# A token recurrence in 64 pairs instead of 56, with its planes stored pair by pair and the order of four engines rewritten around it

## The chip, the cores and the metric

One NeuronCore of a Trainium2 chip runs the whole program in one launch. The metric is device microseconds of one execution. Before the change three runs gave 447.07, 447.06 and 449.86 us, median 447.07 us. The engines are named as in the profile: PE (TensorE, with PEld for its weight loads), DVE (VectorE), ACT (ScalarE), POOL (GpSimd) and SP (SyncE, which only issues DMAs here).

## The reference, cut to what matters

1,536 tokens (8 images of 64 patches and 128 text tokens) are embedded, and then pass a recurrent layer, an expert layer with routing, a linear attention and a second expert layer. The change touches the recurrent layer alone:

```
def step(h, xs):
    b_t, d_t, u_t = xs                      # bivector, decay, injection of token t
    h_new = d_t * rodrigues(b_t, h) + u_t   # rotate the 64 3-vectors of a sequence, scale, add
    return h_new, h_new
_, states = scan(step, 0, tokens 0..191)    # 8 sequences of 192 tokens
```

`b_t`, `d_t` and `u_t` are projections of the layer-normed token. One step is an affine map of a 3-vector, so it can be written as a 3x4 matrix: nine entries from the rotation (through a quaternion) times the decay, and the injection as the fourth column. The map of two neighbouring tokens together is again one 3x4 matrix.

## The kernel before, in words

The 512 chains (8 sequences x 64 vectors) lie as 128 partitions x 4 (`NCH`). Time is cut into three chunks of 64 tokens (`TCH`): chunk 0 holds the patches, chunks 1 and 2 the text. For each chunk the planes bivector, angle, sine, cosine, quaternion and at last the entries of the matrices are computed with 256 elements a partition for a plane. `Mt` holds the matrices, `entries(c, sl)` is the view through which planes are written into it.

The work is spread over engines by a hand-written order; semaphores tie it together.

- **Chunk 0** is DVE's (L1303 to L1331): angles, reciprocal (`recip_of`, L536), products of two planes at a time, and at the end seven instructions that write the nine rotation entries (L1326, L1329, L1330). The last raises `m_ready` to 1.
- **Chunks 1 and 2** start with the projections on PE (`project`, L2110), copies of the bivector on ACT (L916), the squares (`squares_of`, L493, ACT), two additions on POOL (`theta2`, L486), the sigmoid's end on POOL (L685, for both chunks at once), square roots, sine and cosine on ACT, the quaternion on POOL (`quaternion`, L663). PE then adds up the entries in PSUM (`assemble`, L2192: the diagonal group first, then three off-diagonal groups in banks 5, 6 and 4), and ACT copies them into `Mt` (`keep_diagonal`, `keep_off`), which raises `m_ready`.
- **The recurrence** is DVE's, and serial. One step (`product` and `total`, L1342 to L1356) is four small instructions, two for each half of the chains: multiply the matrix entries by the state, and reduce. The states stand in a ring of two PSUM banks, and ACT copies every 32 of them to `hist` (`keep_states`). `steps` does one token each. `pair_steps` does two tokens each, with composed matrices: 0 to 79 were single steps and the other 112 tokens were 56 pairs in seven blocks of eight (`PBLK`), 136 steps in all.
- **The composed matrices** of a block come from POOL, which multiplies the terms (L715, nine instructions a block), PE, which sums them in PSUM (`pair_sums`, L2175), and ACT, which copies them (`keep_pairs`, L956, raises `pair_ready`). DVE waits for `pair_ready` at the head of each block.
- **The odd tokens** that a pair skips are filled in afterwards: the first 41 by POOL in three groups (L722 to L729), the last 15 by DVE (L1413, L1417).
- **What follows** needs all states: PE transposes them back into rows (L2270) once `odd_ready` (POOL and DVE) and `hist_copied` are complete; then come the layer norm, the routing and the experts.

`keep_busy` (L1870) issues matmuls whose result nobody reads. One count of them stands in front of `assemble`: 24 at L2172. The layer norm of the last four text tiles is four ACT instructions (`ln_norm(1, 2, h)`, L904); the text projections need them.

Of the kernel before, what the change touches and what calls it, by code (L numbers as in the profile page):

```python
# [29 lines left out]
ALU = mybir.AluOpType  # L30
# [3 lines left out]
P = 128  # L34
# [3 lines left out]
NJ = NTOK // P  # L38
# [26 lines left out]
PBLK = (8,) * 7  # L65
# [36 lines left out]
def build(nc, x, out):  # L102
    ctx = ExitStack()
    with ctx:
# [112 lines left out]
        Mt = mraw.rearrange("p (t a r c) -> p t a r c", a=NCH, r=3, c=4)  # L217

        Mf = mraw.rearrange("p (t a e) -> p e a t", a=NCH, e=12)
        hist = carve(reg1, (T + 1) * NCH * 4).rearrange("p (a c t) -> p t a c", a=NCH, c=4)  # L220
        biv = carve(reg1, 3 * NCH * T).rearrange("p (c a t) -> p c a t", c=3, a=NCH)
        dec = carve(reg1, NCH * T).rearrange("p (a t) -> p a t", a=NCH)
        U = NCH * TCH

        def unit(v, n):
            return v.rearrange("p (c a t) -> p c a t", c=n, a=NCH)
# [29 lines left out]
        ODD = (0, 8, 24, 41)  # L256
# [18 lines left out]
        comp += [of_pairs(setA.v.rearrange("p c a t -> p (c a t)"), 0, PBLK[6])]  # L275
        PAIR_BANK = (0, 6, 7, 4, 5, 6, 7)
        dodd = of_pairs(setA.trig.rearrange("p c a t -> p (c a t)"), 0, PAIRS - NODD)
# [93 lines left out]
        xn_ready = sem("xn_ready"); xn5_ready = sem("xn5_ready")  # L371
# [61 lines left out]
        biv0 = psum[:, 2 * 512:2 * 512 + 3 * U].rearrange("p (c a t) -> p c a t", c=3, a=NCH)  # L433
        dec0 = psum[:, 4 * 512 + 3 * U:6 * 512].rearrange("p (a t) -> p a t", a=NCH)
        inj0 = psum[:, 4 * 512:4 * 512 + 3 * U].rearrange("p (c a t) -> p c a t", c=3, a=NCH)
# [3 lines left out]
        RECIP_AT = 18  # L439
# [34 lines left out]
        b3 = [P, 3, NCH, TCH]  # L474

        def chunk(v, c):
            return v[..., c * TCH:(c + 1) * TCH]

        def dec2(c, n):

            return chunk(dec, c).unsqueeze(1).to_broadcast([P, n, NCH, TCH])

        def entries(c, sl):
            return Mf[:, sl, :, c * TCH:(c + 1) * TCH]
# [78 lines left out]
        def _(sp):  # L563
# [26 lines left out]
            sp.wait_ge(xn_ready, NJ)  # L590
# [15 lines left out]
            for g in range(3):  # L606
                js = slice(4 * g, 4 * g + 4)
                sp.wait_ge(xn_ready, NJ + 4 * g + 4)
                sp.dma_start(tok_rows(xd[0], 1)[:, js, :], xn[:, js, :]).then_inc(xd_written, 16)
# [31 lines left out]
        def _(pool):  # L641
# [13 lines left out]
            G = nc.gpsimd  # L655
            def angle_left(c):
# [6 lines left out]
            def quaternion(c):  # L663
# [9 lines left out]
                G.tensor_tensor(S.v, chunk(biv, c), S.fq[:, 0:1].to_broadcast(b3), ALU.mult).then_inc(v_ready, 1)  # L673
                pool.wait_ge(v_ready, c)
# [4 lines left out]

            theta2(G, pool, link, 1)  # L680
# [3 lines left out]
            late = dec[:, :, NPATCH:T]  # L684
# [3 lines left out]
            quaternion(1)  # L688
            angle_left(2)


            pool.wait_ge(rsum_ready, 1)
# [10 lines left out]
            quaternion(2)  # L703


            for b, n in enumerate(PBLK):
                i0 = PAIR0 + 2 * sum(PBLK[:b])
                first, second = Mt[:, i0:i0 + 2 * n:2], Mt[:, i0 + 1:i0 + 2 * n:2]
                pool.wait_ge(m_ready, (i0 + 2 * n - 1) // TCH + 1)
                if b == 0:  # L710
                    pool.wait_ge(ev_act, 8)
                if b >= 2:
                    pool.wait_ge(pair_mm, b - 1)
                for k in range(3):
                    for r in range(3):  # L715
                        ins = nc.gpsimd.tensor_tensor(term[b % 2][k][:, 0:n, :, r, :],  # L716
                                                      second[:, :, :, r, k:k + 1].to_broadcast([P, n, NCH, 4]),
                                                      first[:, :, :, k, :], ALU.mult)
                    ins.then_inc(term_ready, 1)
# [1837 lines left out]
```

## Time and the profile before

| | us |
|---|---|
| median of three runs | 447.07 |
| the profiled execution | 444.51 |
| its span (first to last instruction) | 442.7 |
| PE busy | 411.5 |
| DVE busy | 288.7 |
| ACT busy | 230.6 |
| POOL busy | 219.5 |
| DMA's share of the chain that ended last | 23% of the span |

Times in the rows are us from the span's start; a row of the timeline gives start, duration, engine, line, operation, output and inputs, and in brackets the idle time before it with what ended it. Instructions of one line that follow each other are merged ("x4"). PE's filler matmuls count as busy, so its busy share says little; the chain that ended last can be followed back only to 215 us, so what happens to the recurrence is read from the timeline of each engine between 25 and 115 us.

### The profile page before, as it was taken

The numbers are of one execution on the slowest core, as the hardware profiler recorded it, in microseconds if no ns is written. First come the engines' busy times: TensorE is split into PE (matmuls) and PEld (weight loads), VectorE is DVE, ScalarE is ACT, GpSimd is POOL, SyncE is SP. The second block draws the span as 40 slices with busy tenths as digits, with TensorE's granted clock in tenths as the row PEclk, the third lists the DMA queues.
The fourth block names the chain that finished last, engine by engine and source line by source line (L and its number), as shares of the span: only waits on it lengthen the run. The fifth ranks groups of instructions, "written<-read, shape, count | busy, mean of one in ns | idle before, by whom it ended". The sixth has DMA issues, their size and how long they took to land.

```text
span 442.7 us, 10871 instructions
## 1 busy us (share of the span) xinstructions
PE 411.5 (93%) x3803; PEld 302.7 (68%) x3803; DVE 288.7 (65%) x1345; ACT 230.6 (52%) x427; POOL 219.5 (50%) x260
## 2 busy tenths in 40 slices
PE   9999998989879999999889889968999999999993
PEld 6653755637535666666534469635999999999993
DVE  6789999999883444444496248995465565565651
ACT  1487845441764555555235203754666666665650
POOL 5303797798045677774400001425556657566534
PEclk9999699999989999999889999988999999999998
DMA  8709300010132222221299993093233333333313
GB/s 234 107 17 250 69 1 2 1 36 1 64 112 62 64 72 73 72 72 44 87 293 230 225 224 117 18 191 108 52 53 54 58 62 52 60 59 52 51 21 36
DMA packets 38584, 38.27 MB, mean 86 GB/s; under 512 B 7331, under 2 KB 35793, under 8 KB 38517
## 3 DMA queue, kind: packets, MB, share of 16 engines
q1 hardware_dynamic: 27601, 22.84, 22.5%
q0 software_dynamic: 9024, 13.44, 16.0%
q10 hardware_dynamic: 1906, 1.30, 1.0%
q8 instruction: 31, 0.51, 0.5%
q14 instruction: 22, 0.18, 0.1%
HBM read 27.72 MB, written 10.53 MB: 86 GB/s over the span
## 4 chain that ended last, share of the span: by engine, by line
DMA 23%; PE 12%; DVE 8%; issue 5%; ACT 2%; POOLq 1%; POOL 1%; DVEq 0%; ACTq 0%
DMA out<-a,idx 21%; PE bank L2029 2%; DVE h L1701 2%; PE bank L2308 1%; PE bank L1874 1%; PE bank L2068 1%; DVE st L1218 1%; PE bank L2417 1%; PE bank L2340 1%; DMA a<-expert_rows 1%; PE bank L2314 1%; PE bank L2389 1%; ACT reg L1022 1%; PE bank L2362 1%; POOL out L767 1%
## 5 line engine op out<-in xcount | busy, mean ns | idle before, releaser
L767 POOL DMA_INDIRECT out<-a,idx x31 | 50.7, 1634 | 46.3 <-DMA out<-a,idx 32.7
L747 POOL DMA_INDIRECT reg<-xn_rows,idxs x59 | 57.7, 978 | 29.4 <-issue 16.2
L2029 PE MATMUL bank<-reg,xT 64*128 64x128 f32 x1116 | 69.0, 275 | 1.3 <-DVE reg L1618 1.3
L2029 PEld LDWEIGHTS bank<-reg,xT 64*128 64x128 f32 x1116 | 65.0, 188 | 1.4 <-DVE reg L1618 1.4
L2068 PE MATMUL bank<-reg 64*128 64x192 f32 x744 | 65.4, 323 | 0.0
L2068 PEld LDWEIGHTS bank<-reg 64*128 64x128 f32 x744 | 59.8, 187 | 0.0
L1874 PE MATMUL bank<-con 128*128 128x512 bf16 x201 | 54.1, 428 | 0.0
L1054 ACT ACTIVATE reg<-reg 128x1152 f32 x31 | 36.1, 1163 | 33.8 <-PE bank L2068 33.8
L1645 DVE TENSOR_SCALAR a<-bank,gs 128x192 f32<-128x192 f32 x31 | 12.9, 417 | 53.3 <-PE bank L2068 53.3
L1874 PEld LDWEIGHTS bank<-con 128*128 128x128 bf16 x201 | 21.4, 110 | 27.3 <-issue 11.5
L755 POOL DMA_INDIRECT expert_rows<-a,idx x28 | 27.6, 987 | 22.0 <-DVE a L1642 21.7
L1642 DVE COPY a<-bank 128x192 f32<-128x192 f32 x28 | 10.0, 357 | 40.7 <-PE bank L2061 40.7
L1073 ACT ACTIVATE xT<-reg 97x576 f32 x28 | 19.1, 682 | 31.1 <-PE bank L2061 31.1
L2012 PE MATMUL bank<-reg,xTs 96*64 (+1 forms) x112 | 33.2, 419 | 0.4 <-DVE xTs L1608 0.4
L2015 PE MATMUL bank<-xT,xTs 96*64 96x288 f32 (+1 forms) x112 | 33.2, 419 | 0.0
L1618 DVE TENSOR_SCALAR reg<-bank,gb 128x128 f32<-128x128 f32 x93 | 32.3, 403 | 0.0
L2058 PE MATMUL bank<-reg 96*64 x168 | 31.9, 326 | 0.0
L2061 PE MATMUL bank<-xT,reg 96*64 96x192 f32 x168 | 31.9, 326 | 0.0
L716 POOL TENSOR_TENSOR reg<-reg 128x128 f32<-128x128 f32 x63 | 26.1, 454 | 5.2 <-PE bank L2189 4.9
L796 POOL TENSOR_SCALAR onep<-rs 128x3 f32<-128x3 f32 x4 | 0.9, 230 | 56.0 <-DVE nm L1230 56.0
L2058 PEld LDWEIGHTS bank<-reg 96*64 96x64 f32 x168 | 22.7, 136 | 7.7 <-issue 0.4
L1037 ACT ACTIVATE reg<-bank 128x384 f32<-128x384 f32 x31 | 15.2, 491 | 18.9 <-PE bank L2029 18.9
(370 smaller groups left out, 880.1 us busy)
## 6 DMA issues: line engine op xcount, KB each, us to landing
reg<-in_w2b SPq DMA_DIRECT2D x8, 576.0 KB, 10.6
reg<-in_w1b SPq DMA_DIRECT2D x8, 288.0 KB, 10.7
reg<-in_w1a SPq DMA_DIRECT2D x8, 216.0 KB
reg<-in_w2a SPq DMA_DIRECT2D x8, 216.0 KB
xn_rows<-xn SPq DMA_DIRECT2D x4, 384.0 KB, 2.8
reg<-in_w1b SPq DMA_DIRECT2D x8, 192.0 KB, 8.2
xn_rows<-xn SPq DMA_DIRECT2D x1, 1152.0 KB, 7.2
out<-h SPq DMA_DIRECT2D x1, 1152.0 KB
```

The lines of the kernel that those rows point to most:

```text
L747: pool.indirect_dma_start(xs[:, i % RING, 0:(D, D2)[l]], None, xd[l], bass.IndirectOffsetOnAxis(ap=idxs[:, i:i + 1], axis=0)).then_inc(xs_ ...
L755: pool.indirect_dma_start(ybuf, bass.IndirectOffsetOnAxis(ap=idx2[:, i:i + 1], axis=0), ys[:, i % YRING, :], None).then_inc(scat[i % YRING ...
L767: pool.indirect_dma_start(out, bass.IndirectOffsetOnAxis(ap=idx2[:, i:i + 1], axis=0), ys[:, i % YRING, :], None, compute_op=ALU.add).then ...
L1054: nc.scalar.activation(w2r[:, p, :], w2b.rearrange("p e c n -> p (e c n)")[:, bass.ds(e * W2R, W2R)], ACT.Copy).then_inc(w2r_act, 1)
L1618: ins = V.tensor_scalar(dst[:, k], src[:, :, 64 * k:64 * k + 64], gb2[:, 0, k:k + 1], gb2[:, 1, k:k + 1], ALU.mult, ALU.add)
L1874: MM(bank[bk][:, :], con[:, 0:P // 2].bitcast(BF16), con[:, 0:2 * P].bitcast(BF16), start=True, stop=True)
L2012: MM(bank[2 + p][0:GR, 0:hid], xTs[0:r, p, k, 0:GR], w1v[0:r, bass.ds(e * (NK * hid) + k * hid, hid)], start=(k == 0), stop=(k == NK - 1))
L2015: ins = MM(bank[2 + p][GR:P, 0:hid], xTs[0:r, p, k, GR:P], w1u[0:r, i % 3, k * hid:(k + 1) * hid], start=(k == 0), stop=(k == NK - 1))
L2029: ins = MM(bank[2 + 2 * p + a][:, c * P:(c + 1) * P], w1r[rs, p, col:col + hc], xT64[rs, p, k, :], start=(c == 0 and k == 0), stop=(c == n ...
L2058: MM(bank[6 + p][0:GR, 0:D], hTs[0:r, p, c * P:c * P + GR], w2v[0:r, bass.ds(e * (nhc * D) + c * D, D)], start=(c == 0), stop=(c == nhc - 1))
L2061: ins = MM(bank[6 + p][GR:P, 0:D], hTs[0:r, p, c * P + GR:(c + 1) * P], w2u[0:r, i % 2, c * D:(c + 1) * D], start=(c == 0), stop=(c == nhc ...
L2068: ins = MM(bank[Y_BANKS[i == NT - 1][a]][:, 0:D], hT2[rs, p, c * P:(c + 1) * P], w2r[rs, p, c * D:(c + 1) * D], start=(c == 0), stop=(c == ...
```

## The change

It does these things at once:

1. `PBLK` becomes eight blocks, so that tokens 0 to 63 are single steps and the other 128 are 64 pairs: 128 steps. POOL fills in the first 49 odd tokens, DVE still the last 15.
2. `Mt`, the bivector, the decay and the planes are stored pair by pair (pair, chain, token of the pair), through the order in which PE's projections read `xT`. A plane's 256 elements are then written with one stride of 12 elements, where they had strides of 12 and 48. POOL's nine terms of a block become three instructions of 384 elements.
3. POOL takes the four layer-norm instructions of the last text tiles from ACT; `xnp_ready` counts them.
4. ACT no longer waits for chunk 0's matrices before it squares chunk 1; it waits for them before it squares chunk 2. The copies of the injections, the roots and the copies of pairs and states are put in another order.
5. POOL does chunk 2's quaternion, then the terms of the first two pair blocks, then chunk 2's products, two more blocks, the routing base, and the last four blocks.
6. PE sums the first two pair blocks between chunk 2's diagonal group and its off-diagonal groups. The wait for three injection copies before `assemble` becomes a wait for one, and each off-diagonal bank waits for its own. The fillers before `assemble` fall from 24 to 2, another count from 12 to 2.
7. DVE's two reciprocals for chunks 1 and 2 stand at steps 12 and 30, where both stood at 18. The patches' rows follow pair block 1, the statistics' end follows block 2.

```diff
-PBLK = (8,) * 7
+PBLK = (8,) * 8
-        ODD = (0, 8, 24, 41)
+        ODD = (0, 16, 32, 49)
-        RECIP_AT = 18
+        RECIP_AT = (12, 30)
 # POOL
+            pool.wait_ge(rstd_ready, ln_sem(1, 2))
+            for j in GROUPS[1][2]:
+                G.tensor_scalar(xn[:, j, :], h[:, j, :], rstd[:, j:j + 1], nmr[:, j:j + 1], ALU.mult,
+                                ALU.add).then_inc(xnp_ready, 1)
...
+            quaternion(2)
+            pair_terms(0)
+            pair_terms(1)
+            products(2)
+            pair_terms(2)
+            pair_terms(3)
             pool.wait_ge(rsum_ready, 1)
...
+            for b in range(4, len(PBLK)):
+                pair_terms(b)
 # a block's terms
-                    for r in range(3):
-                        ins = nc.gpsimd.tensor_tensor(term[b % 2][k][:, 0:n, :, r, :],
-                                                      second[:, :, :, r, k:k + 1].to_broadcast([P, n, NCH, 4]),
-                                                      first[:, :, :, k, :], ALU.mult)
+                    every = [P, n * NCH, 3, 4]
+                    nc.gpsimd.tensor_tensor(term[b % 2][k][:, 0:n].rearrange("p i a r c -> p (i a) r c"),
+                                            second[:, :, :, k:k + 1].to_broadcast(every),
+                                            first[:, :, k:k + 1, :].to_broadcast(every),
+                                            ALU.mult).then_inc(term_ready, 1)
 # ACT
-            ln_norm(1, 2, h)
+            xt_evac(4)
+            xt_evac(5)
             cosine_of(act, link, 0)
...
-            act.wait_ge(m_ready, 1)
             act.wait_ge(ev_biv, 3)
             squares_of(act, 1)
-            squares_of(act, 2)
...
             theta_of(act, 1)
+            act.wait_ge(m_ready, 1)
+            squares_of(act, 2)
...
             keep_diagonal(2)
+            keep_pairs(0)
+            keep_pairs(1)
             keep_off(2)          # keep_states(1) stands inside, before its second copy
+            keep_pairs(2)
+            keep_states(2)
+            keep_pairs(3)
             xt_evac(NPAIR)
             xt_evac(NPAIR + 1)
             ln_std(2, 0)
 # DVE
-            steps(TCH, PAIR0 - TCH)
             pair_steps(0)
+            pair_steps(1)
 # PE
-            keep_busy(24, 1)
-            pe.wait_ge(ev_act, 8)
+            keep_busy(2, 1)
+            pe.wait_ge(ev_act, 6)
...
+                if c == 2:
+                    pair_sums(0)
+                    pair_sums(1)
                 pe.wait_ge(vv_ready, c)
                 for r, (bk, minus) in enumerate(((5, 0), (6, 0), (4, 1))):
+                    if c == 1:
+                        pe.wait_ge(ev_act, 7 + min(r, 1))
+                    elif r == 1:
+                        pe.wait_ge(pair_ready, 2)
...
             pe.wait_ge(xT_ready, XT_BASE[2] + 2)
-            pe.wait_ge(pair_ready, 5)
+            pe.wait_ge(pair_ready, len(PBLK))
```

## Rows read from the trace of the kernel before

**Rows 1.** Windows of 20 us, all engines: busy (instructions), then granted clock
```profile
60.00:80.00 20.00, 18.26 (x64) 11.22 (x62) 19.30 (x180) 10.22 (x13) 16.46 (x29) 1.00 0.01 2
```
**Rows 2.** Timeline of DVE through the recurrence, from the first step to the odd tokens
```profile
39.34 0.26 DVE L1349 TENSOR_TENSOR reg<-reg,bank 128x18 f32<-128x18 f32 x2
...
39.77 0.26 DVE L1349 TENSOR_TENSOR reg<-reg,bank 128x18 f32<-128x18 f32 x2
...
71.26 0.26 DVE L1349 TENSOR_TENSOR reg<-reg,bank 128x18 f32<-128x18 f32 x2
...
78.88 0.26 DVE L1349 TENSOR_TENSOR a<-a,bank 128x18 f32<-128x18 f32 x2 [0.64 <-ACT a L959]
...
92.65 0.26 DVE L1349 TENSOR_TENSOR a<-a,bank 128x18 f32<-128x18 f32 x2 [0.48 <-ACT a L959]
...
106.68 1.02 DVE L1413 TENSOR_TENSOR reg<-reg,bank 128x240 f32<-128x240 f32 x3
107.73 0.90 DVE L1417 TENSOR_REDUCE reg<-reg 128x180 f32<-128x720 f32 x1
```
**Rows 3.** Timeline of POOL, its last odd group
```profile
109.27 0.56 POOL L729 TENSOR_TENSOR reg<-reg 128x204 f32<-128x204 f32 x1
```
**Rows 4.** Timeline of PE, the states' way back into rows
```profile
109.98 3.18 PE L2270 MATMUL bank<-reg 128*128 128x144 f32 x24 [0.94 <-issue]
```
**Rows 5.** Timeline of ACT, chunk 1's last entries copied
```profile
66.79 1.04 ACT L968 ACTIVATE reg<-bank 128x512 f32<-128x512 f32 x1 [0.66 <-PE bank L2223]
```
**Rows 6.** Timeline of PE, the fillers before the assembly
```profile
50.83 6.89 PE L1874 MATMUL bank<-con 128*128 128x512 bf16 x24
```
**Rows 7.** Groups of POOL's instructions by shape: line, form, count, busy us, mean ns
```profile
L716 POOL TENSOR_TENSOR reg<-reg 128x128 f32<-128x128 f32 x63 | 26.1, 454 | 5.2 <-PE bank L2189 4.9 <-ACTq L973 0.3
...
L801 POOL TENSOR_SCALAR h<-h,onep,nm 128x192 f32<-128x192 f32 x12 | 6.0, 512 | 5.1 <-ACT xn L885 5.1
...
L728 POOL TENSOR_TENSOR reg<-reg 128x384 f32<-128x384 f32 x1 | 0.8, 828 | 0.1
```
**Rows 8.** Timeline of POOL, its work between the embedding and the angles
```profile
39.84 0.73 POOL L490 TENSOR_TENSOR reg<-reg 128x256 f32<-128x256 f32 x1 [24.29 <-ACT reg L495]
...
41.35 1.94 POOL L685 TENSOR_SCALAR reg<-reg 128x512 f32<-128x512 f32 x1
```
**Rows 9.** Timeline of DVE, chunk 0
```profile
25.16 0.29 DVE L1303 TENSOR_SCALAR reg<-reg 128x256 f32<-128x256 f32 x1
...
31.61 0.43 DVE L1320 SCALAR_TENSOR_TENSOR reg<-reg 128x256 f32<-128x256 f32 x1 [0.47 <-ACT reg L907]
...
38.30 0.58 DVE L1330 TENSOR_TENSOR reg<-reg 128x256 f32<-128x256 f32 x1
```
**Rows 10.** Timeline of ACT: layer norm of the last text tiles, squares
```profile
28.36 1.85 ACT L843 ACTIVATE xn<-h,nmr,rstd 128x192 f32<-128x192 f32 x4
...
38.91 1.58 ACT L495 ACTIVATE reg<-reg 128x768 f32<-128x768 f32 x2 [0.37 <-DVE reg L1330]
```
**Rows 11.** Timeline of DVE, one operation beside POOL and later alone
```profile
109.50 0.37 DVE L1442 TENSOR_TENSOR lgs<-lgs,rstd 128x32 f32<-128x32 f32 x1
...
116.72 0.22 DVE L1442 TENSOR_TENSOR lgs<-lgs,rstd 128x64 f32<-128x64 f32 x1
```
**Rows 12.** Timeline of POOL and of DVE in one stretch of the second routing
```profile
287.36 0.60 POOL L801 TENSOR_SCALAR h<-h,onep,nm 128x192 f32<-128x192 f32 x1
...
287.39 0.28 DVE L1471 TENSOR_TENSOR ex<-lgs,mx 128x96 f32<-128x96 f32 x1
287.60 0.40 DVE L1472 TENSOR_TENSOR ex<-mx 128x24 f32<-128x24 f32 x1
```
**Rows 13.** Timeline of ACT, the patches' standard deviation
```profile
86.85 0.30 ACT L830 ACTIVATE std<-mv,con 128x4 f32<-128x4 f32 x1
```
**Rows 14.** Timeline of PE: fillers of the first routing
```profile
121.06 3.61 PE L1874 MATMUL bank<-con 128*128 128x512 bf16 x16
```
**Rows 15.** A window of 1 us: PE busy (instructions), granted clock, DMA
```profile
129.00:130.00 1.00, 1.00 (x5) 0.53 0.08 16
```

## What the change does to the time, predicted before it ran

> **What bounds the kernel now.** The windows over the span come first: from 60 to 80 us DVE works 19.3 of 20 us, and the other engines less, fillers on PE left aside [rows 1]. Then the timeline of DVE, to see what that work is. From 39.34 to 106.68 us it is the serial recurrence, one step in 0.43 us (39.34 to 39.77) [rows 2]. In it only two waits are worth naming: 0.64 us before the first pair block and 0.48 us before another, both for ACT's copy of a composed block [rows 2]. Third, the timelines of POOL and PE where the recurrence ends: DVE's last odd token is done at 108.63 (107.73 + 0.90) [rows 2], POOL's only at 109.83 (109.27 + 0.56) [rows 3], and PE starts the way back into rows at 109.98 [rows 4]. So POOL, not DVE, ends this stage, by 1.2 us. Everything after 109.98 follows it in a chain and is not touched by the change; I take it as shifted by whatever that start shifts. The sum below is the shift of this 109.98.
>
> **Steps.** 80 + 56 = 136 steps become 64 + 64 = 128: 8 x 0.43 = **-3.44**. The strides by which a step reads its matrices change, but each run of three or four numbers stays whole; no row has the new stride, and with four instructions a step, 0.01 us each would give 5 us for all 512. I take 0, because the two kinds of step of today, whose matrices lie in different tiles, take the same 0.26 us [rows 2].
>
> **Are the pairs there in time?** DVE stands at token 64 at 71.26 today [rows 2], and it will need block 0 then. Today chunk 1's matrices are complete at 67.83 (66.79 + 1.04) [rows 5], with PE's assembly held behind 24 fillers of 6.89 us until 57.72 [rows 6]; all of it but two fillers goes. Suppose none of this were won. POOL then needs three instructions for block 0, PE one more product and ACT one copy. A term instruction has 384 elements. The nearest rows are 0.83 us for one instruction of 384, and 0.454 us for one of 128, of which three would be 1.36 [rows 7]. I take 0.95, nearer the row of the same size; a block is 2.9 us, so block 0's terms stand at 70.7. PE's 2 x 384 + 2 x 96 columns for the last product cost 0.9 us (L2270 takes 3.18 for 24 x 144 [rows 4]), ACT's copy some 0.5, and chunk 2's diagonal group may stand ahead on PE: block 0 at 72 to 74. With half of the fillers' 6.9 us won it stands at 69 to 71. By the next term DVE arrives at 74.7, so this costs nothing, and the two waits go: -0.64 - 0.48 = **-1.12**. If DVE is not late, block 0 is just in time. The cover is thus the fillers' place and DVE's own lateness.
>
> **A wait that may come.** ACT's standard deviation for the patches is done at 87.15 (86.85 + 0.30) [rows 13]; two more copies are put ahead of it, one of which cannot start until DVE reaches pair block 2, and DVE reads it right behind that block. Between 0 and 0.6 us; I take **+0.3**.
>
> **When the recurrence starts.** This is the term that I am least sure of. Two pieces of POOL's work are moved beside DVE's chunk 0, which today has POOL quiet for 24.29 us, up to 39.84 [rows 8]. What that can do is seen elsewhere: a DVE addition with both inputs in SBUF that started at 109.50, while POOL's instruction ran until 109.83 [rows 3], took 0.37 us and ended at 109.87; on twice as many elements and without POOL it took 0.22 [rows 11]. It waited for POOL to end. DVE's steps, with one input in PSUM, keep their 0.26 us all along [rows 2]. And POOL gets between two DVE instructions that stand one behind the other: at 287.39 one of DVE ran, POOL's took 0.60 where such take 0.51 [rows 7], and DVE's next, of 24 elements, ran until 288.00, right behind POOL's end at 287.96 [rows 12]. So I let them take turns.
>
> First piece: the four layer-norm instructions on POOL, 0.51 each [rows 7], come when DVE starts its chain at 25.16 [rows 9], of which five instructions use two inputs or the form of 25.16. At the least they cost nothing, at most 4 x 0.51 = 2.05. I take half, 1.0, less the 0.47 for which DVE waited for ACT at 31.61 [rows 9] and which goes as ACT is freed of 1.85 us [rows 10]: **+0.5**.
>
> Second piece: ACT's squares for chunk 1 waited 0.37 us for chunk 0's matrices and began at 38.91 [rows 10]. That wait is gone and the projections come earlier, by 1.85 us of ACT [rows 10] and some 0.3 of fillers. The squares then start at 38.54 - 2.2 = 36.3 and take 0.8 (half of the 1.58 for two), so POOL has its two additions (0.73 each) and the 1.94 of L685 to do from 37.2 on [rows 8]. DVE then is in its last six writes of the matrices, which end at 38.88 today [rows 9] and at 39.4 with the first piece. They use two inputs each, and each POOL instruction can hold one of them. The bounds are 0 and 0.73 + 0.73 + 1.94 = 3.4. In the order worked out here all three fall in, with about half a us of the last one's margin: **+2.9**, since a part of each overlaps the DVE instruction before it. DVE's writes themselves, 0.58 with strides against 0.43 without [rows 9], could gain from the new stride: 0.15 for each of the six and three times that for the one of 768 elements, 1.35 at most; I take 0, as they still go one number at a time. Together the recurrence starts at 39.34 + 3.4 = 42.7, and token 64 is at 74.7.
>
> The Trainium skill (SBUF — State Buffer, Who interferes with whom) says that a VectorE instruction with two SBUF inputs and a GpSimd instruction that reads SBUF exclude each other, and that the second to come is blocked until the first is over. The trace agrees as to who is blocked [rows 11], and by the whole length of each instruction the start would be 5.0 later instead of 3.4; it is a rival below.
>
> **The end of the stage.** POOL has 24 term instructions of 0.95 = 22.8 us where 63 took 26.1 [rows 7], starts them some us earlier, and has eight more odd tokens to fill, about 1.2 us. With DVE's own last token at 108.63 + 3.4 - 3.44 - 1.12 + 0.3 = 107.8, POOL should be done first, and its 1.2 us of today goes: **-1.1**. At 1.36 a term it would have 24 x 0.41 = 9.8 us more to do and end some us later than today.
>
> **Sum**: -3.44 - 1.12 + 0.3 + 0.5 + 2.9 - 1.1 = -2.0 us. The profiled execution took 444.51 us (its span 442.7) and would take 442.5; it lies 2.6 us under the median of 447.07, against which the forecast stands: **445.0 us**.
>
> **The rivals.**
> - *POOL misses chunk 0.* If DVE is half a us earlier or POOL's adds half a us later, L685 finds DVE done, and the start is 0.5 to 1.7 late instead of 3.4: -3.7 to -4.9, so 442.2 to 443.4. For it: margins of half a us, and the writes' new stride. Against it: the times above.
> - *PE's clock falls before the way back.* PE now waits for all eight blocks, then does everything else and waits for DVE; it has little work for some 3 us before L2270. After the fillers that ended at 124.67 [rows 14] PE had little to do, and from 129 to 130 the granted clock was 0.53, most of it at 1.2 GHz [rows 15]; today's gap before L2270 is 0.94 [rows 4]. At 1.2 GHz the 3.18 of L2270 double: +3.2, to 448.2. No row has a gap between these two.
> - *POOL stays last.* With terms at 1.15, 4.8 us more in all, POOL's end, which I put some 3 us ahead of DVE's 107.8, falls at 109.6 and the rest is saved for nothing: -0.3, so 446.8.
> - *The whole lock.* Each of the seven POOL instructions holds DVE for its length: 2.05 + 3.4 - 0.47 = 5.0, and 446.7.
> - *Slower: the assembly at half clock.* The 24 fillers stand behind small matmuls. If the clock is at 1.2 GHz there and the assembly does not raise it as the fillers did, chunk 1's assembly, 57.7 to 66.8 today [rows 5, 6], takes 18 us instead of 9, from 50.8 on: matrices at 70. Chunk 2's diagonal group, four tenths of such an assembly by its columns, takes 7.2 instead of 3.6, block 0's sums (2,500 columns, 2.3 us by [rows 4]) 4.6, and block 0 comes at about 82. It decides where block 0 lands over 2 us behind DVE's 74.7; at 82 it costs 7.3, so -2.0 + 7.3 = +5.3: 452.4. Against it: the assembly is dense work like the fillers.
>
> **How the numbers follow.** The forecast has 0.38. POOL missing chunk 0 has 0.25, the fallen clock 0.17, POOL last 0.08, the whole lock 0.06, the half-clock assembly 0.06. About 1% (4.4 us) is what a measurement of this kernel can tell from no change. Faster by more needs 442.6 or less: the better part of the first rival and some luck with the forecast, 0.18. Slower by more is the last rival: 0.06. Within 1%: 0.76. The range from 441.6 to 448.6 takes in all but the last rival and the best end of the first.
>
> **What would show it.** DVE's first step at 42.7 and not 39.3; L1326 to L1330 stretched, each right behind a POOL instruction's end; `theta2` on POOL at 37 to 39. No wait of DVE at the first pair block; a short one at the statistics' end for ACT. Term instructions of 0.95 us, POOL's last odd group before DVE's, and PE's L2270 right behind DVE's L1417. The granted clock before L2270 tells the second rival; block 0's copy against DVE's arrival tells the last. The forecast is wrong where the recurrence starts within a us of today's, or where DVE waits at token 64.

## The result, and the profile after

The changed kernel takes 443.38 us (median of 20 runs, 440.97 to 446.47) where the kernel before takes 446.81 us (median of 20, 444.30 to 449.86). The ratio is 0.9926, with a 95% interval of 0.9906 to 0.9946: 3.3 us less, or 0.7%. That is within the 1% that the prediction set as its limit, and 1.6 us under the 445.0 that it gave. The profiled execution took 443.01 us, its span is 441.2 us (before 442.7).

The timeline of DVE in chunk 0 of the changed kernel comes first (start, duration, engine, line; compare [rows 9]).

```profile
25.80 0.29 DVE L1325 TENSOR_SCALAR reg<-reg 128x256 f32<-128x256 f32 x1
26.12 0.50 DVE L1326 TENSOR_SCALAR reg<-reg 128x256 f32<-128x256 f32 x1
...
27.29 0.61 DVE L1329 SCALAR_TENSOR_TENSOR reg<-reg 128x256 f32<-128x256 f32 x1
...
35.51 1.58 DVE L1348 TENSOR_TENSOR reg<-reg 128x768 f32<-128x768 f32 x1
36.93 0.65 DVE L1351 TENSOR_TENSOR reg<-reg 128x256 f32<-128x256 f32 x1
37.42 0.63 DVE L1352 TENSOR_TENSOR reg<-reg 128x256 f32<-128x256 f32 x1
...
39.32 0.62 DVE L1352 TENSOR_TENSOR reg<-reg 128x256 f32<-128x256 f32 x1
40.05 0.31 DVE L1360 MEMSET bank<- 128x128 f32 x2
...
40.41 0.26 DVE L1371 TENSOR_TENSOR reg<-reg,bank 128x18 f32<-128x18 f32 x2
```

Everything is 0.64 us later than before from the first of these rows on (25.80 against 25.16 [rows 9]), ahead of anything that the change touches in this chain; it belongs to the single execution (in the traces of the runs below, whose edits all lie behind this row or beside it, it stands anywhere from 25.25 to 26.59), and times below are counted from this row. The recurrence starts 14.61 us behind it, before 14.18 [rows 2, 9].

The timeline of POOL of the changed kernel, from the layer norm to its last odd group:

```profile
25.98 2.42 POOL L664 TENSOR_SCALAR xn<-h,rstd,nmr 128x192 f32<-128x192 f32 x4 [9.44 <-DVE nmr L1260]
37.88 2.53 POOL L495 TENSOR_TENSOR reg<-reg 128x256 f32<-128x256 f32 x1 [9.48 <-ACT reg L500]
40.49 0.73 POOL L496 TENSOR_TENSOR reg<-reg 128x256 f32<-128x256 f32 x1
...
63.25 5.21 POOL L706 TENSOR_TENSOR reg<-reg 128x384 f32<-128x384 f32 x6
...
103.18 0.56 POOL L753 TENSOR_TENSOR reg<-reg 128x204 f32<-128x204 f32 x1
```

The main row is L495. An addition that takes 0.73 us alone (the row under it) stands there for 2.53 us, and ends at 40.41, when DVE's writes are over. POOL did the waiting, not DVE. The seven runs below that leave these writes and the squares' place alone, and the norms on POOL, show the same: 2.50 to 2.53 us.

DVE's timeline through the recurrence of the changed kernel (compare [rows 2]):

```profile
45.52 0.75 DVE L545 TENSOR_SCALAR reg<-reg 128x256 f32<-128x256 f32 x1
...
55.60 0.81 DVE L545 TENSOR_SCALAR reg<-reg 128x256 f32<-128x256 f32 x1
...
72.74 0.26 DVE L1371 TENSOR_TENSOR a<-a,bank 128x18 f32<-128x18 f32 x2
...
86.47 0.18 DVE L1257 RECIPROCAL rstd<-std 128x4 f32<-128x4 f32 x1 [0.39 <-ACT std L854]
...
104.09 1.02 DVE L1436 TENSOR_TENSOR reg<-reg,bank 128x240 f32<-128x240 f32 x3
105.14 0.91 DVE L1440 TENSOR_REDUCE reg<-reg 128x180 f32<-128x720 f32 x1
```

The first pair block starts at 72.74 without a wait: ACT's timeline has its copy done at 69.57, 3.2 us earlier, and the second block's at 71.84. The two waits of [rows 2] are gone, and one of 0.39 us at L1257 is new.

```profile
69.08 0.49 ACT L980 ACTIVATE a<-bank 128x384 f32<-128x384 f32 x1 [0.73 <-PE bank L2213]
71.35 0.49 ACT L980 ACTIVATE a<-bank 128x384 f32<-128x384 f32 x1 [1.78 <-PE bank L2213]
...
109.41 2.22 ACT L1136 ACTIVATE h<-bank 128x384 f32<-128x384 f32 x3 [0.75 <-PE bank L2299]
```

Last, PE where the stage ends: its timeline (compare [rows 4]) and five windows of 1 us (length, busy and instructions, granted clock, DMA):

```profile
101.26 1.24 PE L1897 MATMUL bank<-con 128*128 128x512 bf16 x5
106.15 4.73 PE L2299 MATMUL bank<-reg 128*128 128x144 f32 x24 [3.65 <-DVE reg L1440]
```
```profile
105.00:106.00 1.00, 0.00 (x0) 0.95 0.00 0
106.00:107.00 1.00, 0.85 (x3) 0.50 0.00 0
107.00:108.00 1.00, 1.00 (x6) 0.50 0.09 16
108.00:109.00 1.00, 1.00 (x6) 0.50 0.00 0
109.00:110.00 1.00, 1.00 (x9) 0.84 0.00 0
```

PE's 24 matmuls start 0.10 us behind DVE's end (106.05) and no longer behind POOL's (103.74). But PE was idle for 3.65 us, its granted clock is 0.50 (1.2 GHz), and the same 24 matmuls take 4.73 us where they took 3.18 [rows 4]. ACT's last copy of rows ends at 111.63; before it ended at 113.89 (110.99 + 2.90 in its timeline).

The ledger, each line from the rows above and [rows 2, 4, 9]:

| stretch | before | after | difference | predicted |
|---|---|---|---|---|
| DVE's chain start to first step | 14.18 | 14.61 | +0.43 | +3.4 |
| first step to DVE's odd tokens | 67.34 | 63.68 | -3.66 | -4.26 |
| DVE's odd tokens to PE's start | 3.30 | 2.06 | -1.24 | -1.1 |
| PE's start to the last row copied | 3.91 | 5.48 | +1.57 | 0 |
| sum | 88.73 | 85.83 | -2.90 | -2.0 |

The sum is near the 3.3 us of the medians. The two profiled executions themselves differ by only 1.5 us in span, as the one of the changed kernel loses 0.64 us ahead of the stage and 0.76 behind its last row (329.6 us there, before 328.8).

### The profile page after: what moved, and what is told of

It reads as the page before. It is cut to its first block, busy times and chain, and to the rows that moved or that the text cites. A ratio compares the mean times of both kernels' runs of the same rounds, so it can differ in the third digit from the quotient of the medians.

```text
span 441.2 us, 10756 instructions
## 1 busy us (share of the span) xinstructions
PE 409.7 (93%) x3779; PEld 304.2 (69%) x3779; DVE 285.9 (65%) x1313; ACT 229.7 (52%) x424; POOL 219.9 (50%) x225
## 4 chain that ended last, share of the span: by engine, by line
PE 26%; DMA 12%; DVE 8%; issue 3%; POOLq 1%; POOL 1%; ACT 0%; DVEq 0%; ACTq 0%
PE bank L2055 9%; PE bank L2094 8%; DMA out<-a,idx 8%; DMA xn_rows<-gate 2%; DVE h L1724 2%; PE bank L2337 1%; DVE st L1240 1%; PE bank L2446 1%; PE bank L2025 1%; PE bank L2418 1%; PE bank L2369 1%; PE bank L2391 1%; DMA a<-expert_rows 1%; PE bank L2343 1%; DMA reg<-xn_rows,idxs 1%
## 5 line engine op out<-in xcount | busy, mean ns | idle before, releaser
L1897 PE MATMUL bank<-con 128*128 128x512 bf16 x169 | 46.3, 431 | 0.0
L1897 PEld LDWEIGHTS bank<-con 128*128 128x128 bf16 x169 | 18.0, 111 | 22.6 <-issue 10.2
L2087 PEld LDWEIGHTS bank<-xT,reg 96*64 96x64 f32 x168 | 22.7, 136 | 0.0
```

The source lines that it names most:

```text
L1897: MM(bank[bk][:, :], con[:, 0:P // 2].bitcast(BF16), con[:, 0:2 * P].bitcast(BF16), start=True, stop=True)
L2087: ins = MM(bank[6 + p][GR:P, 0:D], hTs[0:r, p, c * P + GR:(c + 1) * P], w2u[0:r, i % 2, c * D:(c + 1) * D], start=(c == 0), stop=(c == nhc ...
```

## The experiments

Each is the changed kernel with one edit, if nothing else is said. The table counts from DVE's chain start to ACT's last copy of rows in one profiled execution, as the ledger does; ratios are to the kernel before, run on the same chip, with 95% intervals.

| run | stage, us | median, us | ratio |
|---|---|---|---|
| before | 88.73 | | |
| changed | 85.83 | 443.38 | 0.9926 (0.9906 to 0.9946) |
| links between DVE's writes | 87.98 | 446.05 | 0.9984 (0.9959 to 1.0010) |
| ACT's wait put back | 86.66 | 444.03 | 0.9979 (0.9946 to 1.0011) |
| 18 fillers at the end | 84.29 | 441.47 | 0.9889 (0.9852 to 0.9925) |
| seven pair blocks | 88.90 | 445.82 | 0.9962 (0.9931 to 0.9993) |
| nine term instructions | 89.89 | 446.24 | 0.9988 (0.9963 to 1.0014) |
| 24 fillers at the assembly | 88.65 | 446.28 | 0.9994 (0.9972 to 1.0017) |
| layer norm back on ACT | 88.26 | 445.15 | 0.9987 (0.9964 to 1.0010) |
| 18 fillers, statistics later | 84.62 | 440.18 | 0.9871 (0.9845 to 0.9898) |
| the same, norms last | 83.82 | 440.38 | 0.9878 (0.9856 to 0.9900) |
| the same, reciprocals moved | 82.83 | 439.35 | 0.9843 (0.9819 to 0.9866) |

**Can POOL get in between DVE's writes?**

```diff
-            V.tensor_tensor(entries(0, slice(0, 11, 5)), ...)
+            link(V.tensor_tensor(entries(0, slice(0, 11, 5)), ...))
 ...                # and so for the next five of the six writes
```

> The changed kernel with a semaphore between each two of DVE's last seven writes of chunk 0's matrices (L1348, L1351, L1352), so that each instruction waits for the one before it. Theory (POOL's additions get into SBUF only where DVE's next instruction has a semaphore to wait for; in a run of instructions without one POOL is kept out): POOL's two additions of theta2 and L685 now run among the writes, each near its length alone (0.73, 0.73, 1.94 us) or up to half longer, DVE's writes are stretched, and the first step of the recurrence starts 2 to 3.5 us later than in the changed kernel (40.41): 42.4 to 43.9; the time 2 to 3 us longer. Rival (DVE always goes first against these instructions of POOL, whether it waits or not): the links cost their own gap, some 0.06 us each, POOL's first addition still takes about 2.5 us, and the first step starts 0.3 to 0.5 us later, about 40.8.

DVE's and POOL's timelines of this run:

```profile
38.48 0.63 DVE L1352 TENSOR_TENSOR reg<-reg 128x256 f32<-128x256 f32 x1
39.15 0.92 DVE L1351 TENSOR_TENSOR reg<-reg 128x256 f32<-128x256 f32 x1
40.10 0.91 DVE L1352 TENSOR_TENSOR reg<-reg 128x256 f32<-128x256 f32 x1
41.04 0.79 DVE L1351 TENSOR_TENSOR reg<-reg 128x256 f32<-128x256 f32 x1
41.87 0.62 DVE L1352 TENSOR_TENSOR reg<-reg 128x256 f32<-128x256 f32 x1
```
```profile
38.58 1.00 POOL L495 TENSOR_TENSOR reg<-reg 128x256 f32<-128x256 f32 x1 [9.48 <-ACT reg L500]
39.65 0.86 POOL L496 TENSOR_TENSOR reg<-reg 128x256 f32<-128x256 f32 x1
40.49 2.19 POOL L716 TENSOR_SCALAR reg<-reg 128x512 f32<-128x512 f32 x1
```

POOL's first addition takes 1.00 us instead of 2.53, and three of DVE's writes take 0.92, 0.91 and 0.79 instead of 0.63. So with a semaphore between the writes POOL gets in, as the theory says, and the rival falls. The size was off: the first step comes at 42.95, 16.45 us behind the chain's start, 1.84 later than in the changed kernel and not 2 to 3.5. Of it the links alone are 6 x 0.20 = 1.2 (0.67 from one write to the next at 37.81 and 38.48, where it is 0.47 to 0.49 without links), and POOL's part 0.29 + 0.28 + 0.16 = 0.73. So where the two do alternate, POOL's additions of 0.73 + 0.73 us delay DVE by 0.57, less than half their length, and L716, 1.94 us alone, delays one write by 0.16: DVE's last write (41.87) lies wholly inside it and takes its 0.62. The stage is 2.15 us longer: 1.84 at the first step and 0.85 behind L2299's counterpart, where the clock fell for longer (the 24 matmuls took 5.61 us), less 0.55 in the recurrence.

**What does POOL cost DVE there in the changed kernel?**

```diff
+            act.wait_ge(m_ready, 1)
             act.wait_ge(ev_biv, 3)
             squares_of(act, 1)
```

> The changed kernel with ACT's wait for chunk 0's matrices put back ahead of chunk 1's squares, so that POOL's additions come only once DVE is in the recurrence. Theory (POOL's second piece costs DVE only the 0.3 us by which its writes are longer, and chunk 1 has some 3 us to spare at the first pair block): the first step starts 0.3 us earlier (40.1), the first writes take 1.49 and 0.44 us as in the kernel before, chunk 1's matrices and pair block 0 come 1.5 to 2.5 us later, DVE still finds block 0 there, and the time is 0 to 0.4 us shorter. Rival (the forecast's own reading: POOL and DVE take turns, and POOL's piece costs DVE up to 2.9 us): the first step 2 to 3 us earlier. A third: the cover at the first pair block is smaller than the trace says, then a wait of DVE at token 64 appears and the time is 1 to 2 us longer.

The timelines of DVE and POOL:

```profile
36.13 1.58 DVE L1349 TENSOR_TENSOR reg<-reg 128x768 f32<-128x768 f32 x1
37.55 0.63 DVE L1352 TENSOR_TENSOR reg<-reg 128x256 f32<-128x256 f32 x1
...
41.01 0.26 DVE L1372 TENSOR_TENSOR reg<-reg,bank 128x18 f32<-128x18 f32 x2
```
```profile
41.51 0.73 POOL L495 TENSOR_TENSOR reg<-reg 128x256 f32<-128x256 f32 x1 [12.50 <-ACT reg L500]
```

POOL is quiet until 41.51, and DVE's writes take just as long: 4.88 us from the first write to the first step (36.13 to 41.01), against 4.90 (35.51 to 40.41) with POOL's addition pending. Theory and rival were both wrong on DVE's start. POOL's second piece costs DVE nothing, and the 0.3 us by which the writes are longer than before are left for the new layout: 0.47 from one write to the next, before 0.44. The third expectation was nearer: the cover is small. ACT squares chunk 1 3.0 us later, counted from the chain's start (at 40.58, where the chain starts at 26.41; in the changed kernel at 36.95). DVE still has no wait at token 64, but waits 0.34 us at pair block 2 and 1.36 us instead of 0.39 at L1257. That is 1.31 us more of waiting; L545 takes 0.52 less in this run (0.49 + 0.55), and the stage is 0.83 us longer. So ACT's wait that the change took out is worth that, and not the time at DVE's start.

**Did the clock cost the end of the stage, and how much?**

```diff
             logits()
-            keep_busy(5, 7)
+            keep_busy(18, 7)
```

> The changed kernel with 18 filler matmuls instead of 5 ahead of the way back to rows, 13 x 0.21 = 2.8 us more, which lie in PE's 3.65 us of idle time. Theory (PE's clock fell to 1.2 GHz because it was idle there, and this gave back part of the gain): the granted clock from 106 to 109 is near 1.0 instead of 0.50, the 24 matmuls of L2299 take about 3.2 us instead of 4.73, and the ranking that follows starts 1.3 to 1.7 us earlier; the time 1.3 to 1.7 us shorter, about 442. Rival (the clock falls there whatever the fillers do, or the stage is not on the path): L2299 keeps 4.7 us, or the later work does not move, and the time stays.

The timeline of PE:

```profile
101.91 4.04 PE L1897 MATMUL bank<-con 128*128 128x512 bf16 x18
106.82 3.18 PE L2299 MATMUL bank<-reg 128*128 128x144 f32 x24 [0.86 <-DVE reg L1440]
```

The granted clock stays at 1.00 from 105 to 110, L2299 takes 3.18 us again, the stage is 1.54 us shorter and the median 1.9 us less. Theory confirmed.

**Are the eight steps the gain?**

```diff
-PBLK = (8,) * 8
+PBLK = (8,) * 7
-        ODD = (0, 16, 32, 49)
+        ODD = (0, 8, 24, 41)
...
+            steps(TCH, PAIR0 - TCH)
             pair_steps(0)
```

> The changed kernel with seven pair blocks instead of eight: sixteen single steps from token 64 to 80, as in the kernel before, and all else as changed. Theory (each of the eight steps saved is worth a step of the recurrence, 0.43 us, and nothing else hangs on the number of blocks): DVE's last odd tokens end 3.4 us later (109.5 instead of 106.05), PE's clock may differ, and the time is 3 to 3.5 us longer, so that nearly the whole of the gain measured is the eight steps. Rival (the gain is in the waits that went and in POOL's order, and the steps are given back by the fallen clock): the time is within 1.5 us of the changed kernel.

ACT's copy of the states behind DVE's last step comes 82.39 us after the chain's start instead of 79.42: 2.97 later. That is 8 x 0.43 = 3.44 less the 0.39 of waiting at L1257, which this run does not have. The stage is 3.07 longer and the median 2.4. So the eight steps are the gain, and 0.39 us of it goes into the wait that the change brings. All the rest of the change together, the fallen clock included, is worth nothing in this stage: with seven blocks it is 88.90 us, and 88.73 in the kernel before. The ratio puts this run 0.4% under the kernel before, which the stage's rows do not show.

**Does POOL have time to spare?**

```diff
-                    every = [P, n * NCH, 3, 4]
-                    nc.gpsimd.tensor_tensor(...)         # 384 elements, three to a block
+                    for r in range(3):
+                        ins = nc.gpsimd.tensor_tensor(...)   # 128 elements, nine to a block
```

> The changed kernel with nine term instructions of 128 elements for a pair block, as before the change, instead of three of 384. Theory (an instruction of 384 costs 0.87 us and three of 128 cost 3 x 0.45 = 1.36; at this price POOL would end the stage, as the rival of the forecast says): POOL has 24 x 0.49 = 11.8 us more to do, waits of 2.7 us for PE's sums cover part of it, its last odd group ends 5 to 9 us later than in the changed kernel (103.7) and behind DVE's, and the time is 3 to 7 us longer. Rival (POOL has enough to spare that it does not end the stage): DVE's last odd tokens still end the stage and the time is within 1.5 us of the changed kernel.

The timelines of POOL and PE:

```profile
111.41 0.62 POOL L753 TENSOR_TENSOR reg<-reg 128x204 f32<-128x204 f32 x1
```
```profile
112.19 3.18 PE L2299 MATMUL bank<-reg 128*128 128x144 f32 x24 [1.66 <-issue]
```

POOL ends at 112.03 and holds PE. Counted from the chain's start, POOL ends 7.89 us and PE starts 5.64 us later than in the changed kernel; DVE's waits at pair block 2 (0.60), at the patches' rows (0.50) and at L1257 (1.36) come on the way. The clock did not fall this time, so the stage is 4.06 us longer. The rival falls: without the larger instructions the eight steps would be spent.

**What did the fillers ahead of the assembly do?**

```diff
-            keep_busy(2, 1)
+            keep_busy(24, 1)
```

> The changed kernel with all 24 filler matmuls back ahead of the assembly of chunk 1. Theory (by the trace the assembly without them runs at a granted clock of 0.50 from 48 to 54 and chunk 1 is still in time): the fillers are 5 to 7 us longer, the assembly behind them is at full clock, chunk 1's matrices come 1 to 3 us later, block 0 comes before DVE reaches token 64, later blocks and the statistics make DVE wait 0.5 to 1.5 us; the time 0 to 1.5 us longer. Rival (the early blocks have no cover worth the name): a wait of DVE at token 64, 2 us or more.

The timeline of PE, and one row of DVE:

```profile
48.75 6.81 PE L1897 MATMUL bank<-con 128*128 128x512 bf16 x23 [0.16 <-issue]
55.40 1.02 PE L2231 MATMUL bank<-reg 128*128 128x512 f32 x2
```
```profile
84.21 0.26 DVE L1371 TENSOR_TENSOR a<-a,bank 128x18 f32<-128x18 f32 x2 [0.59 <-ACT a L980]
```

Without the fillers the first two matmuls of the assembly take 2.05 us at 49.66, with the granted clock at 0.50 from 48 to 54; with them 1.02 us at 55.40. The assembly starts 4.95 us later and chunk 1 is complete only 2.4 us later, as the assembly then runs at full clock. DVE has no wait at token 64, but 0.59 us at pair block 2 and 1.36 at L1257, and the stage is 2.82 us longer, more than the 0 to 1.5 expected. The part of it that lies before DVE's odd tokens is 1.86 (80.15 against 78.29); the rest lies behind L2299's start, where the clock fell again and ACT's last copy came 6.44 us later instead of 5.48.

**What is the layer norm on POOL worth?** The four instructions go back to ACT, behind the sine; the two copies `xt_evac(4)` and `xt_evac(5)` stay ahead of the cosine, where the change put them.

> The changed kernel with the third layer norm's four instructions back on ACT. Forecast's reading: on POOL they stretch DVE's instructions from 26 to 28 us by 0.56 and free ACT for 0.47 of DVE's later wait, so alone they are worth about nothing at DVE's start; ACT's squares for chunk 1 come 1.5 to 2 us later. Theory: DVE's first step of the recurrence, counted from the start of its chain (L1325), comes within 0.2 us of the changed kernel's 14.61; chunk 1 comes 1 to 2 us later, DVE waits up to 1 us for later blocks; the time 0 to 1.2 us longer. Rival (the move is what makes chunk 1 early enough): a wait at token 64, 2 us or more longer.

The timeline of DVE:

```profile
25.58 0.29 DVE L1322 TENSOR_SCALAR reg<-reg 128x256 f32<-128x256 f32 x1
...
33.57 0.42 DVE L1338 SCALAR_TENSOR_TENSOR reg<-reg 128x256 f32<-128x256 f32 x1 [2.35 <-ACT reg L929]
```

Without POOL the second instruction is back at 0.29 us, and the chain up to the reciprocal takes 1.78 us (25.25 to 27.03) instead of 2.34, so the 0.56 us of stretch are POOL's. But DVE then waits 2.35 us for ACT's cosine squared: ACT has the norms and the two copies ahead of it. The first step comes 16.34 us behind the chain's start instead of 14.61, and the stage is 2.43 us longer. The expectation of "within 0.2" was wrong, because it left out that the copies had moved ahead too: POOL's piece is what makes room for them.

**A version that is faster than both.**

```diff
-            keep_busy(5, 7)
+            keep_busy(18, 7)
 # DVE
             pair_steps(2)
+            pair_steps(3)
             ln_end(2, 0)
...
 # ACT
-            ln_norm(2, 0, h)
             keep_pairs(5)
+            ln_norm(2, 0, h)
```

> The changed kernel with 18 fillers ahead of the way back, and with DVE's end of the patches' statistics and ACT's layer norm one pair block later, so that DVE does not wait 0.39 us for the standard deviation. Theory: L2299 at 3.2 us behind a granted clock near 1.0, no wait at L1257, and the way back 0.4 us earlier than with the fillers alone: 441.1 median, 2.3 us under the changed kernel's 443.4. Rival (the wait only moves, as ACT's copies of the next blocks come later): as with the fillers alone, 441.5.

The wait at L1257 is gone, and DVE's odd tokens come at 77.86 us behind the chain's start instead of 78.29. But PE came to its fillers 1.4 us late and was still in them when DVE's last token was done, so the stage is 0.33 us longer than with the fillers alone. PE's timeline, with one window of its granted clock (0.50) under it:

```profile
94.76 1.24 PE L2287 MATMUL bank<-h,con 128*128 128x192 f32 x4 [1.10 <-issue]
...
103.41 4.05 PE L1898 MATMUL bank<-con 128*128 128x512 bf16 x18
107.29 3.10 PE L2300 MATMUL bank<-reg 128*128 128x144 f32 x24
```
```profile
98.00:99.00 1.00, 1.00 (x6) 0.50 0.03 8
```

The rows' sums (L2287) begin 0.48 us later than in the changed kernel, counted from the chain's start, as ACT's norms held the last blocks' copies up. The larger part of the 1.4 us is the clock, which was 0.50 from 97 to 100 while PE worked on these sums. The next run was built on the copies alone, with the norms behind the last one:

> As the run with both edits (18 fillers; the patches' statistics one pair block later), but ACT's layer norm of the patches behind the last pair block's copy instead of between blocks 5 and 6. In that run the norms held the last copies up, PE began the rows' sums 1.4 us later than in the changed kernel, and the fillers ended 0.9 us behind DVE's last tokens, at 107.3. Theory (so PE waited for its own fillers): the fillers end before DVE's last tokens again, and L2299 starts right behind DVE, 0.9 us earlier relative to the start of DVE's chain than there (79.9 instead of 80.76): 439.3. Rival (something else held L2299, or a later use of the normed rows is now late): no change or longer, 440.2 or more.

PE's timeline:

```profile
94.96 1.24 PE L2287 MATMUL bank<-h,con 128*128 128x192 f32 x4 [0.63 <-issue]
```

L2300 starts at 106.55, 79.99 us behind the chain's start and 0.19 behind DVE, as expected; the stage is 0.80 us shorter. But the reason is another than the one given: the sums begin no earlier than in the run before (68.40 us behind the chain's start, there 68.23), and this time the granted clock stays at 1.00 through them. That the shorter idle time ahead of them (0.63 us, there 1.10) kept it up is not shown. The median (440.38) lies where the rival had put it (440.2 or more), and the two runs' intervals overlap nearly whole. Then the reciprocals, with `RECIP_AT = (14, 37)` and 14 fillers:

> The run before with the two reciprocals at steps 14 and 37 instead of 12 and 30, and 14 fillers instead of 18, as DVE is expected earlier. At steps 12 and 30 the additions L545 ahead of the reciprocals took 0.73 and 0.83 us where such take 0.28, and each time POOL was in an instruction of two inputs (46.11 to 46.83, 56.95 to 57.72); at 14 and 37 POOL is idle, waiting for ACT or for the reciprocal itself. Theory (an instruction of DVE that needs what POOL holds waits until POOL's is over, whole): L545 takes 0.28 us both times, the recurrence is 0.9 to 1.0 us shorter, and if nothing else is late the time is 0.9 us less, 438.4. Rival (0.73 and 0.83 are the cost of that place in the recurrence, or chunk 2's later reciprocal makes its matrices late): L545 stays at 0.7 or more, or DVE waits at a pair block, and the time stays.

DVE's timeline with 12 and 30 (the first of these three kernels), and then with 14 and 37:

```profile
46.25 0.73 DVE L545 TENSOR_SCALAR reg<-reg 128x256 f32<-128x256 f32 x1
...
56.31 0.83 DVE L545 TENSOR_SCALAR reg<-reg 128x256 f32<-128x256 f32 x1
```
```profile
46.26 0.29 DVE L545 TENSOR_SCALAR reg<-reg 128x256 f32<-128x256 f32 x1
...
58.02 0.28 DVE L545 TENSOR_SCALAR reg<-reg 128x256 f32<-128x256 f32 x1
```

0.29 and 0.28 us, no wait at a pair block, and DVE's odd tokens 0.97 us earlier than in the run before (76.87 against 77.84). The expectation names the wrong instruction of POOL for the second: what L545 met at 56.31 was the end of a product of 1.80 us (L692, 55.19 to 56.99), not the addition that began at 56.95. Median 439.35, ratio 0.9843: the best version, 1.6% under the kernel before.

## Why the prediction was right, point by point

The time came out within the range and on the side forecast. But two large terms were wrong in opposite directions, and that they nearly cancel is luck. What the sum stands for, the shift of PE's start, was forecast at -2.0 and came out at -4.47 (+0.43 - 3.66 - 1.24); the fallen clock, which was a rival and no term, gave 1.57 back. And one of the prediction's own signs of being wrong is there: counted from the start of DVE's chain, the recurrence starts within a us of the kernel before's, 0.43 later.

- **Steps, -3.44, and the two waits, -1.12: right.** From the first step to the odd tokens the difference is -3.66 = -3.44 - 1.12 + 0.39 + 0.51. The 0.39 is the new wait for the standard deviation, predicted at +0.3. The 0.51 was not in the sum: the instructions L545, ahead of the reciprocals at steps 12 and 30, take 0.75 + 0.81 us where the two at step 18 took 0.37 + 0.68, as each fell into an instruction of POOL. The run with the reciprocals moved shows it. That moved instructions meet POOL was worked out for chunk 0, and not for these two.
- **The pairs in time: right.** A term instruction takes 0.87 us (5.21 / 6), assumed 0.95. Block 0 is there at 69.57; the prediction had 69 to 71 with half of the fillers' time won.
- **The recurrence's start, +3.4: wrong, +0.43.** The first piece was nearly nothing: 0.56 us of stretch less the 0.47 wait that went, +0.12 up to L1342, predicted +0.5. The step that failed is the second piece, "I let them take turns", +2.9. In both places from which it was read POOL's instruction was under way first: 109.27 before DVE's 109.50 (a multiplication, not the addition that the prediction calls it) [rows 3, 11], 287.36 before 287.39 [rows 12]. Here DVE was: its last seven writes stand back to back with no semaphore between them, the third was running, and POOL did not get a turn. Its addition came as foreseen (37.88, with this execution's 0.64; "from 37.2 on") and waited for all four that were left. The links showed it from one side (POOL in, DVE later), ACT's wait put back from the other (POOL absent, DVE no earlier). The price was wrong too: where the links gave POOL its turns, they cost DVE 0.73 us and not 2.9. How far the rule reaches is open, as L1471 and L1472 [rows 12] have no semaphore between them either, and there POOL did hold up the second. What is left of the term is +0.3, which the prediction had put at 0 with a gain possible; POOL is not its cause, and the new layout of the writes is what remains, though no run took it back alone.
- **The end of the stage, -1.1: right, -1.24.** POOL is 2.3 us ahead of DVE. With nine instructions a block it would not be.
- **The clock rival came true beside the forecast.** It was given 0.17 and 3.2 us; PE's idle time was 3.65 us, the clock fell, and it cost 1.57 us, about half. The clock was back at 0.84 from 109 to 110, before the last of the 24 matmuls ended; that is why doubling 3.18 was too much. The price is not fixed: in the run with 24 fillers at the assembly, behind 3.35 us of idle time, the clock was 0.50 from 108 to 113 and the same matmuls took 5.71 us.
- **The other rivals.** "POOL misses chunk 0" had the right start of the recurrence, and its 442.2 to 443.4 takes in the 443.38 measured, but for another reason: POOL was there and was kept out. "The whole lock" and "POOL stays last" did not happen. "The assembly at half clock" did in part: 0.50 from 48 to 54 us, but 1.00 from 55 on, while the assembly ran, so chunk 1 was complete at 62.5 and not at 70. The kernel before had 0.50 from 48 to 53 as well, ahead of its fillers and in them.

With the measured sizes in their places the sum would be -2.0 - 2.97 (start) + 0.51 (reciprocals) + 0.09 (the wait) - 0.14 (POOL) + 1.57 (clock) = -2.94, the ledger's -2.90 but for rounding.

What stays open: single runs of one kernel differ by up to 5.5 us (440.97 to 446.47 for the changed one), more than most edits here are worth. Much of it goes with PE's clock: of these 20 runs the four fastest have a mean granted clock of 0.964 or 0.965, the three slowest 0.950 to 0.953. In the traces the clock falls behind the stage too, and not each time: from 10 to 20 us behind ACT's last copy of rows its mean is 0.66 in the run with 18 fillers (443.67 us) and 1.00 in the one with the statistics later (439.74 us). That this is the cause no run shows. So the verdicts on small edits rest on the stage's rows, each from one execution; against the changed kernel the medians agree with them in sign, but not between the runs with 18 fillers, where steps of +0.33 and -0.80 us by the rows are -1.29 and +0.20 in the medians. The run with the wait put back is another poor match: +0.83 us by its rows, and +2.4 by the ratios, with a wide interval.

## What to carry to other kernels

Where two engines get in each other's way, ask not only what each instruction holds but whether the other can get in: here a run of instructions that wait for nothing kept it out, the same run with semaphores let it in, and a lone instruction paid for what it met. When DVE's stage gets shorter, look at what PE does while it waits: thirteen more fillers in that gap gave 1.5 us, beside the 2.9 that the change had won. And a step put into a full schedule should be placed where the engine that it contends with is waiting for somebody else: two constants, 12 and 30 made into 14 and 37, were worth 1.0 us.

## What the runs showed of the hardware that was not expected

- An addition of POOL with two inputs, at 37.88, took 2.53 us instead of 0.73 beside DVE's back-to-back two-input writes, and those lost 0.02 us by it (4.90 against 4.88). The Trainium skill (SBUF — State Buffer, Who interferes with whom) has the two exclude each other, the first to start holding the path for its instruction. For POOL's additions the traces agree: with the links, each held up the write that came behind it. They do not agree for "its instruction" in the case of L716: in the run with links DVE's write at 41.87 took its 0.62 us wholly inside it (40.49 to 42.68). Which of the two comes next when DVE's following instruction is ready at once, the runs show for these writes.
- A DVE instruction with one input from SBUF also waits for POOL: L545 took 0.28 or 0.29 us with POOL idle, 0.73 where it met an addition of POOL early (46.11 to 46.83 for the row at 46.25), 0.83 where it met the second half of a product of 1.80 us (55.19 to 56.99 for the row at 56.31), and 1.43 us where it met nearly the whole of such a one, in the run with the norms on ACT (55.79 to 57.59, L545 from 56.32 to 57.75). Each time it ended some 0.15 us behind POOL's instruction. The recurrence's own steps, with one input in PSUM, kept 0.26 us throughout.
- The same idle time of PE ended at two clocks. Ahead of L2299 it was idle for 1.59 us in the run with seven blocks, and the granted clock was 0.53 in the window from 109 to 110; it was idle for 1.66 us in the run with nine terms, and the clock was 1.00 and the 24 matmuls took 3.18 us. At 0.86 and 0.30 us the clock held, at 3.35 and 3.65 it fell. What decides between 1.59 and 1.66 is open. Nor need the fall come in the idle time: with the statistics later it came between 96 and 97, when PE had been at work again since 94.76.
- Writes of 256 elements, one every 12 elements with one stride, take 0.47 us from one to the next; with the two strides of before it was 0.44. The simpler pattern was not the faster one; that the stride is the reason is argued, not shown.
